# Feature products of one sample each on 32-column quarters, and one table gathered instead of three

## The chip, the cores and the metric

The kernel runs on one core of a Trainium2 chip. The metric is the device time of one execution in microseconds; the median of three runs of the kernel before is 417.11 us (416.43 to 417.47). The engines in the profile are PE (TensorE's matmuls), PEld (its weight loads, which can overlap the matmuls), DVE (VectorE), ACT (ScalarE), POOL (GpSimd) and SP (SyncE).

## The reference

For each of 2048 samples, 26 embedding rows of 128 numbers are looked up and set beside one dense row; all 351 pairwise dot products of these 27 vectors go, with the dense row, through a three-layer network.

```python
e = jnp.stack([tbl_0[ids[:, 0]], ..., tbl_25[ids[:, 25]]], axis=1)      # 2048 x 26 x 128
combined = jnp.concatenate([e, dense_x[:, None, :]], axis=1)            # 2048 x 27 x 128
interact = jnp.einsum('bfd,bgd->bfg', combined, combined)
z = interact[:, _TRIU_I, _TRIU_J]                                       # 351 pairs
h = jnp.concatenate([z, r_dense_x], axis=1)                             # 479
h = jnp.maximum(h @ W_top1 + b_top1, 0.0)                               # 512
h = jnp.maximum(h @ W_top2 + b_top2, 0.0)                               # 256
y = h @ W_top3
```

All inputs are float32. Seven tables have 1000 rows, ten 1250, eight 12500 and one 125000.

## The kernel before

The batch is worked on in 8 blocks of 256 samples, each of two tiles of 128. All features of a sample end up in `xt` (partitions: the 128 numbers of a row; free: sample, then feature slot, 32 slots for a sample). There are two ways into it.

**Gathered features.** POOL issues one indirect DMA for each (tile, table) (L577), which puts 128 table rows into `raw`. PE turns them with a transpose against `ident` (L594, `turn` steps, up to four tables in one PSUM bank), and ACT copies the bank into `xt` (L821). `SHARES` says how many of the ten small ("hot") tables are gathered in each block beside the 16 large ones: none in block 0, three in blocks 1 to 7. That makes 298 gathers.

**One-hot features.** The other hot tables lie in SBUF, cut into chunks of 128 rows (8 chunks for a table of 1000 rows, 10 for 1250), as a rounded part `hot_hi` and a residue `hot_lo`. DVE compares the block's ids with row numbers (L874, `onehot`, up to four chunks of 256 samples in one instruction, a ring of `RING = 3` such pieces), and PE multiplies each chunk by its one-hot columns (L613, one product with `hot_hi`, one with `hot_lo`; the first use of some tables takes `hot_in` as float32, `direct`). ACT copies the sum into `xt` (L387). Each table of a block is an "item", each item is two or three "pieces".

**Feature products.** For four samples at once PE takes the 128 columns of `xt` (four samples times 32 slots) as weights and the 4 x 27 columns as the moving side (L629). The result has 128 x 108 numbers, of which only the four diagonal blocks are wanted. Four such products fill a bank of `gram_ps` (two banks). `gram_copy` (L402 to L412) takes the four diagonal blocks out with four copies of 32 partitions, one for each sample of a group, on ACT; for the last tile two of the four are DVE's. A tile has 8 fills (`n_gram`), so 128 in all. A float32 matmul shows as two records and two weight loads in the trace, so 512 products are 1024 records.

**Tail.** For each block the pairs are turned and packed (L653, L424, L428), turned again (L661), and multiplied by the weights (L684, L690). In blocks 0 to 6 these steps are spread among the next block's steps; for the last block they come at the end (L712 to L775).

**What sets the order.** `order` is one list of steps (`hot`, `turn`, `gram`, `held`, `tail`), made from slots (L181 to L230). Every engine walks this same list and does its part of each step, waiting on semaphores for the others. `gram_slots` (L173) puts one fill of products and two slots of hot pieces in turn. `pieces_made` (L241) says after which step DVE makes which one-hot piece: at most `RING` ahead of use, one at a `gram` step. `copied_no` and `x_free` hold PE back until ACT has emptied one of three banks `x_ps`. POOL walks its own list of gathers: it waits for the landing of all but the last two gathers of the burst of eight before (`burst_landed`), and for the turn that frees its part of `raw`. The weights' rounding on ACT (`round_at`), their residue on DVE (`split_at`), and the residues of the direct tables (`split_late`) are hung on steps of the list.

## Time and profile before

| | |
|---|---|
| median of three runs | 417.11 us |
| the profiled execution | 417.3 us |
| its span, first to last instruction | 415.5 us |
| granted TensorE clock | 1.00 throughout |
| busy: PE / PEld | 393.7 us (95%) / 367.4 us (88%) |
| busy: POOL / ACT / DVE | 288.6 us (69%) / 264.6 us (64%) / 185.9 us (45%) |

Busy time is the union of an engine's records. A matmul's record reaches from its start to its modelled end, and the next one starts long before that, so the busy share says little about how fast PE goes; the distance between two starts does. It is worked out here from a timeline row of n records: (length of the row minus the length of one record) / (n - 1). POOL's busy time leaves out about 0.3 us between two gathers, in which it waits for nothing that the profile shows.

### The profile page before, as it was taken

How to read it: one execution, taken by the hardware profiler on the slowest of the kernel's cores; microseconds unless marked ns; L12 is line 12 of the kernel's file. 1: busy time of each engine (PE TensorE's matmuls, PEld its weight loads, DVE VectorE, ACT ScalarE, POOL GpSimd, SP SyncE). 2: the span in 40 equal slices, each digit the busy share in tenths (PEclk: the TensorE clock that was granted, in tenths of full speed). 3: DMA queues.
4: the chain of work that ended last, by engine and by line, in shares of the span. 5: the costliest groups of instructions: out<-in, count | busy, mean ns of one | idle time of the engine just before them, and what ended most of it. 6: DMA issues, size and time to landing. Idle time of an engine off the chain costs nothing.

```text
span 415.5 us, 8094 instructions
## 1 busy us (share of the span) xinstructions
PE 393.7 (95%) x3094; PEld 367.4 (88%) x3094; DVE 185.9 (45%) x216; ACT 264.6 (64%) x915; POOL 288.6 (69%) x306
## 2 busy tenths in 40 slices
PE   3899999999999999999999999999999999989997
PEld 2678899899899989998999989998999989889886
DVE  5796868441546224541447134451447124401142
ACT  2351377868586766767585766757485766866532
POOL 6776787777777777777777777777777777777000
PEclk9999999999999999999999999999999999999999
DMA  6788333212313222122222232312212222122000
GB/s 179 228 239 245 111 102 98 58 44 66 84 51 77 56 65 78 52 83 64 53 81 54 52 90 59 77 52 69 77 52 56 79 64 54 52 53 56 6 2 2
DMA packets 18231, 32.43 MB, mean 78 GB/s; under 512 B 6120, under 2 KB 9072, under 8 KB 18192
## 3 DMA queue, kind: packets, MB, share of 16 engines
q0 software_dynamic: 9536, 19.55, 18.3%
q1 hardware_dynamic: 7776, 11.57, 9.0%
q10 hardware_dynamic: 880, 0.80, 0.7%
q8 instruction: 25, 0.41, 0.4%
q14 instruction: 14, 0.11, 0.1%
HBM read 31.88 MB, written 0.01 MB: 77 GB/s over the span
## 4 chain that ended last, share of the span: by engine, by line
POOL 54%; issue 24%; PE 11%; DMA 9%; ACT 1%; POOLq 0%; ACTq 0%
POOL raw L577 54%; DMA raw<-in_tbl,ids_sb 9%; PE gram_ps L629 4%; PE tail_ps L684 2%; PE tail_ps L661 1%; PE tail_ps L653 1%; PE x_ps L721 1%; DMA ids_sb<-in_ids 1%; PE x_ps L594 1%; PE x_ps L613 0%; PE tail_ps L732 0%; PE x_ps L715 0%; PE x_ps L716 0%; PE x_ps L725 0%; PE gram_ps L774 0%
## 5 line engine op out<-in xcount | busy, mean ns | idle before, releaser
L577 POOL DMA_INDIRECT raw<-in_tbl,ids_sb x298 | 287.7, 966 | 95.3 <-issue 88.0
L874 DVE TENSOR_TENSOR onehot<-ids_wide,row_ps 128x1024 fp32r<-128x1024 int16 (+1 forms) x121 | 143.9, 1206 | 108.6 <-PE x_ps L613 107.7
L411 ACT COPY gram<-gram_ps 32x104 f32<-32x104 f32 x496 | 117.8, 237 | 46.0 <-PE gram_ps L629 38.3
L629 PE MATMUL gram_ps<-xt 128*128 128x108 f32 x1024 | 129.2, 276 | 2.2 <-ACT xt L821 1.0
L629 PEld LDWEIGHTS gram_ps<-xt 128*128 128x128 f32 x1024 | 121.9, 191 | 5.3 <-ACT gram L411 1.3
L613 PE MATMUL x_ps<-onehot,hot_hi 128*128 128x256 f32 x416 | 110.5, 299 | 7.4 <-ACT xt L387 6.4
L613 PE MATMUL x_ps<-onehot,hot_lo 128*128 128x256 f32 x416 | 103.2, 281 | 0.0
L613 PEld LDWEIGHTS x_ps<-onehot,hot_hi 128*128 128x128 f32 x416 | 78.4, 189 | 14.5 <-ACT xt L387 10.8
L613 PEld LDWEIGHTS x_ps<-onehot,hot_lo 128*128 128x128 f32 x416 | 78.6, 189 | 0.0
L387 ACT COPY xt<-x_ps 128x128 f32<-128x128 f32 (+1 forms) x80 | 36.0, 504 | 34.6 <-PE x_ps L613 34.1
L821 ACT COPY xt<-x_ps 128x512 f32<-128x512 f32 (+1 forms) x78 | 48.1, 679 | 1.3 <-PE x_ps L594 1.3
L594 PE MATMUL x_ps<-ident,raw 128*128 128x128 f32 x298 | 39.6, 275 | 1.1 <-DMA raw<-in_tbl,ids_sb 0.8
L613 PE MATMUL x_ps<-onehot,hot_in 128*128 128x256 f32 x124 | 30.1, 400 | 6.8 <-DMA hot_in<-in_tbl 6.8
L594 PEld LDWEIGHTS x_ps<-ident,raw 128*128 128x128 f32 x298 | 33.3, 141 | 3.1 <-ACT xt L821 1.5
L473 DVE TENSOR_TENSOR h_lo<-h,h_hi 128x256 fp32r<-128x256 f32 x28 | 12.0, 429 | 51.9 <-ACT h L445 51.8
L613 PEld LDWEIGHTS x_ps<-onehot,hot_in 128*128 128x128 f32 x124 | 24.4, 201 | 10.7 <-issue 7.3
L468 DVE TENSOR_TENSOR zt_lo<-tail_ps,zt_hi 118x256 fp32r<-118x256 f32 (+2 forms) x24 | 10.2, 424 | 40.3 <-ACT zt_hi L440 40.2
L684 PE MATMUL tail_ps<-zt_hi,weights_hi 118*128 118x256 f32 (+2 forms) x84 | 26.0, 336 | 0.0
L684 PE MATMUL tail_ps<-zt_hi,weights_lo 118*128 118x256 f32 (+2 forms) x84 | 21.7, 284 | 0.0
L424 ACT COPY z<-tail_ps 128x100 f32<-128x100 f32 (+12 forms) x99 | 13.5, 230 | 10.7 <-PE tail_ps L653 10.6
L444 ACT ACTIVATE h_hi<-tail_ps,b_sb 128x256 fp32r<-128x256 f32 x28 | 13.3, 475 | 9.8 <-PE tail_ps L684 9.0
L785 ACT CAST hot_hi<-hot_in 128x1024 fp32r<-128x1024 f32 x7 | 7.3, 1047 | 16.9 <-DMA hot_in<-in_tbl 16.9
(76 smaller groups left out, 317.6 us busy)
## 6 DMA issues: line engine op xcount, KB each, us to landing
raw<-in_tbl,ids_sb POOLq DMA_INDIRECT x298, 2.6
hot_in<-in_tbl SPq DMA_DIRECT2D x14, 256.0 KB, 3.3
ids_wide<-in_hot_ids SPq DMA_DIRECT2D x14, 256.0 KB, 3.4
hot_in<-in_tbl SPq DMA_DIRECT2D x6, 320.0 KB, 4.0
weights_in_place<-in_w SPq DMA_DIRECT2D x10, 128.0 KB, 2.7
dense_sb<-in_dense_t ACTq DMA_DIRECT2D x6, 128.0 KB, 2.5
dense_sb<-in_dense_t SPq DMA_DIRECT2D x2, 128.0 KB, 3.5
w1d_sb<-in_w SPq DMA_DIRECT2D x2, 128.0 KB
```

The source lines that it names most:

```text
L387: last = copy(xt[:, place:place + (b - a) * P, feature], src[:, a * P:b * P])
L411: last = copy(gram[rows, :, per_fill * i:per_fill * (i + 1)], src)
L424: copy(z[:, :, pair_start[q // 2]:pair_start[q // 2 + 1]], src)
L444: nc.scalar.activation(h1_hi[:, j, :], ps[:, 0:BLOCK], ACT.Relu, bias=bias).then_inc(h1_rounded, 1)
L473: nc.vector.tensor_tensor(h1_lo[:, j, :], h1[:, j, :], h1_hi[:, j, :].bitcast(F32), ALU.subtract).then_inc(h1_split, 1)
L577: nc.gpsimd.indirect_dma_start(out=raw[k][:, f, :], out_offset=None, in_=sources[f], in_offset=bass.IndirectOffsetOnAxis(ap=ids_sb[:, t, f ...
L594: last = nc.tensor.transpose(ps[:, c * P:(c + 1) * P], raw[k][:, f, :], ident[:, :])
L613: last = nc.tensor.matmul(ps, table[:, chunk_at[j] + c, :], moving[:, c - a, :], start=(c == 0 and table is tables_of[0]), stop=(c == chun ...
L629: last = nc.tensor.matmul(gram_ps[m % 2][:, col:col + QUAD * feats], xt[:, b:b + QUAD, :].rearrange("p b f -> p (b f)"), xt[:, b:b + QUAD, ...
L684: last = nc.tensor.matmul(ps[:, 0:BLOCK], weights, moving, start=(n == 0), stop=(n == len(products_of) - 1))
L821: copy(xt[:, b:b + P, fs[0]:fs[-1] + 1], src).then_inc(x_copied, 1)
L874: nc.vector.tensor_tensor(columns(p), ids_wide[:, it // IDS % IDS_RING, it % IDS, 0:width].unsqueeze(1).to_broadcast([P, n, width]), row_n ...
```

## The change

A product now takes one sample: 27 columns of `xt` as weights, 26 as the moving side, and its result goes to partitions 32s to 32s+26 of the bank for the sample s of its group of four, so that it uses one 32-column quarter of the array. There are 2048 such products, 4096 records. A bank now holds 16 groups (16 x 26 = 416 columns), a tile has 2 fills, and one copy of 128 partitions takes a whole fill (for the last tile one of 64 partitions on ACT and one on DVE). The rows that no product writes are set to 0 once by DVE, in the two PSUM banks, where before unused slots of `xt` were. The hot pieces among the products stand in two stretches for a tile.

`SHARES` goes from 3 to 1 for blocks 1 to 7: 270 gathers instead of 298, and two more hot tables of 1250 rows (20 chunks) by one-hot products in each of these seven blocks. `pieces_made` may make three pieces at a `gram` step. The residues of the direct tables and the splits of the weights hang on other `gram` steps.

```diff
--- before.py
+++ after.py
@@ -14,10 +14,11 @@
 BLOCK = 256
 SLOTS = 32
 QUAD = 4
+FILLS = 2
 BANK = 512
 HOT = 10
 DIRECT = 5
-SHARES = (0, 3, 3, 3, 3, 3, 3, 3)
+SHARES = (0, 1, 1, 1, 1, 1, 1, 1)
 MOST = max(SHARES)
 RAW = 2
 DENSE = 2
@@ -83,9 +84,9 @@
         count = -(-n // 4)
         turn_groups.append([list(range(g * n // count, (g + 1) * n // count)) for g in range(count)])
     most_turns = max(len(gs) for gs in turn_groups)
-    per_fill = BANK // (QUAD * feats)
-    n_gram = groups // per_fill
-    assert n_gram * per_fill == groups
+    per_fill = groups // FILLS
+    n_gram = FILLS
+    assert per_fill * (feats - 1) <= BANK
     gram_block = tiles_block * n_gram
 
 
@@ -172,8 +173,8 @@
 
     def gram_slots(t, hot=()):
 
-        return [[("gram", t * n_gram + i)] + [step for slot in hot[(i - 1) * len(hot) // n_gram:(i + 1) * len(hot) // n_gram]
-                                              for step in slot if i % 2] for i in range(n_gram)]
+        cut = [i * len(hot) // n_gram for i in range(n_gram + 1)]
+        return [[("gram", t * n_gram + i)] + [step for slot in hot[cut[i]:cut[i + 1]] for step in slot] for i in range(n_gram)]
 
 
 
@@ -247,7 +248,7 @@
             end = min(used + RING + 1, len(pieces))
             coming = [s[0] for s in order[n + 1:] if s[0] in ("gram", "hot")][:1]
             if step[0] == "gram":
-                end = min(end, nxt + 1)
+                end = min(end, nxt + 3)
             elif coming == ["gram"]:
                 end = nxt
             made.append(list(range(nxt, max(nxt, end))))
@@ -319,7 +320,7 @@
 
         second = [("gram", gram_block + n) for n in range(len(weight_parts) - n_kz)]
         round_at = [("hot", item_start[nh + 2 + n]) for n in range(n_kz)] + second
-        split_at = [("gram", n_gram + 1 + 2 * n) for n in range(n_kz)] + second
+        split_at = [("gram", n_gram + n // 2) for n in range(n_kz)] + second
 
         x_ps = [psum(f"x_ps{b}", [P, BANK]) for b in range(3)]
         row_ps = psum("row_ps", [P, BANK])
@@ -346,13 +347,13 @@
         consts_ready = sem("consts_ready")
         hot_rounded = sem("hot_rounded")
         hot_split = sem("hot_split")
-        xt_cleared = sem("xt_cleared")
         row_no_ready = sem("row_no_ready")
         piece_ready = sem("piece_ready")
         piece_used = sem("piece_used")
         turn_full = [sem(f"turn_full{k}") for k in range(RAW)]
         x_copied = sem("x_copied")
         dense_copied = sem("dense_copied")
+        gram_cleared = sem("gram_cleared")
         gram_full = sem("gram_full")
         gram_copied = sem("gram_copied")
         gram_shared = sem("gram_shared")
@@ -404,12 +405,9 @@
             h, i = divmod(m, gram_block)
             if i == 0:
                 reach(eng, tail_full["cols"], h * n_cols)
-            for s in quads:
-                rows = slice(32 * s, 32 * s + 32)
-                src = gram_ps[m % 2][rows, 0:per_fill * QUAD * feats].rearrange(
-                    "p (g c) -> p c g", g=per_fill)[:, s * feats:(s + 1) * feats - 1, :]
-                last = copy(gram[rows, :, per_fill * i:per_fill * (i + 1)], src)
-            last.then_inc(done, 1)
+            rows = slice(SLOTS * quads[0], SLOTS * (quads[-1] + 1))
+            src = gram_ps[m % 2][rows, 0:per_fill * (feats - 1)].rearrange("p (g c) -> p c g", g=per_fill)
+            copy(gram[rows, :, per_fill * i:per_fill * (i + 1)], src).then_inc(done, 1)
 
         def product_copied(eng, m):
 
@@ -623,12 +621,14 @@
                     pe.wait_ge(x_copied, max(copied_no[step] for step in of_tile))
                     pe.wait_ge(dense_copied, t // tiles_block + 1)
                 product_copied(pe, m - 2)
+                if m == 0:
+                    pe.wait_ge(gram_cleared, len(gram_ps))
                 for g in range(per_fill):
-                    b = t % XT * P + (i * per_fill + g) * QUAD
-                    col = g * QUAD * feats
-                    last = nc.tensor.matmul(gram_ps[m % 2][:, col:col + QUAD * feats],
-                                            xt[:, b:b + QUAD, :].rearrange("p b f -> p (b f)"),
-                                            xt[:, b:b + QUAD, 0:feats], start=True, stop=True)
+                    cols = slice(g * (feats - 1), (g + 1) * (feats - 1))
+                    for s in range(QUAD):
+                        b = t % XT * P + (i * per_fill + g) * QUAD + s
+                        last = nc.tensor.matmul(gram_ps[m % 2][SLOTS * s:SLOTS * s + feats, cols],
+                                                xt[:, b, 0:feats], xt[:, b, 0:feats - 1], start=True, stop=True)
                 last.then_inc(gram_full, 1)
 
             def tail_has(kind, h):
@@ -787,8 +787,6 @@
             def hot_copy(it):
                 j, first, n = items[it]
                 act.wait_ge(piece_used, item_end[it])
-                if it == 0:
-                    act.wait_ge(xt_cleared, 1)
 
                 to_xt(copy, first, n, nf + j, x_ps[fill_no["hot", it] % len(x_ps)]).then_inc(x_copied, 1)
                 if it == (it - j_th[it] + last_item[first] + 1) // 2:
@@ -881,19 +879,20 @@
             for n in row_kinds:
                 copy(row_no[n], row_sb[n][:, :]).then_inc(row_no_ready, 1)
             dve.wait_ge(row_no_ready, len(row_kinds))
-            nc.vector.memset(xt[:, :, feats:], 0.0).then_inc(xt_cleared, 1)
+            for ps in gram_ps:
+                nc.vector.memset(ps[:, :], 0.0).then_inc(gram_cleared, 1)
             for (kind, *what), made in zip(order, pieces_made()):
                 if kind == "tail":
                     h, key, part = what
                     if part == parts[key] - 1:
                         tail_split(dve, h, key)
                 elif kind == "gram":
-                    if what[0] < len(split_late):
-                        hot_residue(split_late[what[0]])
+                    if what[0] < n_gram:
+                        for j in split_late[what[0] * len(split_late) // n_gram:(what[0] + 1) * len(split_late) // n_gram]:
+                            hot_residue(j)
                     if what[0] >= shared_from:
                         gram_copy(dve, copy, gram_shared, (2, 3), *what)
-                    if (kind, *what) in split_at:
-                        n = split_at.index((kind, *what))
+                    for n in [n for n, at in enumerate(split_at) if at == (kind, *what)]:
                         hi, lo, src = weight_parts[n]
                         dve.wait_ge(weights_rounded, n + 1)
                         nc.vector.tensor_tensor(lo, src, hi.bitcast(F32), ALU.subtract).then_inc(weights_split, 1)
```

**PE, one-hot products and feature products in block 0's second tile.** L613 are one-hot products, L629 feature products of four samples. Before:

```order
L613 MATMUL x_ps<-onehot,hot_lo 128x256
L629 MATMUL gram_ps<-xt 128x108 x8
L613 MATMUL x_ps<-onehot,hot_hi 128x256
L613 MATMUL x_ps<-onehot,hot_lo 128x256
L613 MATMUL x_ps<-onehot,hot_hi 128x256
L613 MATMUL x_ps<-onehot,hot_lo 128x256
L613 MATMUL x_ps<-onehot,hot_hi 128x256
L613 MATMUL x_ps<-onehot,hot_lo 128x256
L613 MATMUL x_ps<-onehot,hot_hi 128x256
L613 MATMUL x_ps<-onehot,hot_lo 128x256
L629 MATMUL gram_ps<-xt 128x108 x8
L613 MATMUL x_ps<-onehot,hot_hi 128x256
```

After, from the middle of the same place (L611 are one-hot products, L630 feature products of one sample):

```order
L611 MATMUL x_ps<-onehot,hot_lo 128x256
L611 MATMUL x_ps<-onehot,hot_hi 128x256
L611 MATMUL x_ps<-onehot,hot_lo 128x256
L630 MATMUL gram_ps<-xt 27x26 x64
L611 MATMUL x_ps<-onehot,hot_hi 128x256
L611 MATMUL x_ps<-onehot,hot_lo 128x256
L611 MATMUL x_ps<-onehot,hot_hi 128x256
L611 MATMUL x_ps<-onehot,hot_lo 128x256
L611 MATMUL x_ps<-onehot,hot_hi 128x256
L611 MATMUL x_ps<-onehot,hot_lo 128x256
L611 MATMUL x_ps<-onehot,hot_hi 128x256
```

Eight products of four samples stood between eight one-hot products; now 64 products of one sample stand in one run, with 24 one-hot products between two runs.

**PE, second tile of a later block, at the end of the z transposes (L661).** Before:

```order
L629 MATMUL gram_ps<-xt 128x108 x4
L661 MATMUL tail_ps<-ident,z 118x64 x4
L629 MATMUL gram_ps<-xt 128x108 x4
L661 MATMUL tail_ps<-ident,z 128x64 x4
L661 MATMUL tail_ps<-ident,z 105x64 x4
L629 MATMUL gram_ps<-xt 128x108 x4
L661 MATMUL tail_ps<-ident,z 64x64 x4
L629 MATMUL gram_ps<-xt 128x108 x8
```

After:

```order
L661 MATMUL tail_ps<-ident,z 128x64 x4
L661 MATMUL tail_ps<-ident,z 105x64 x4
L630 MATMUL gram_ps<-xt 27x26 x64
L661 MATMUL tail_ps<-ident,z 64x64 x4
L630 MATMUL gram_ps<-xt 27x26 x64
L592 MATMUL x_ps<-ident,raw 128x128 x3
```

The tile's two runs of 64 products have four transposes between them, and no one-hot products.

**ACT, copies out of PSUM in a first tile (L411 and L410: feature products; L387 and L388: one-hot sums).** Before:

```order
L387 COPY xt<-x_ps 128x256
L411 COPY gram<-gram_ps 32x26x4 x16
L387 COPY xt<-x_ps 128x256
L387 COPY xt<-dense_sb 128x256
L411 COPY gram<-gram_ps 32x26x4 x16
```

After:

```order
L388 COPY xt<-x_ps 128x256
L410 COPY gram<-gram_ps 128x26x16
L388 COPY xt<-x_ps 128x256
L388 COPY xt<-dense_sb 128x256
L410 COPY gram<-gram_ps 128x26x16
```

Sixteen copies of 32 partitions between two other copies became one of 128 partitions.

## Rows read from the trace of the kernel before

**Rows 1.** The page: granted clock in tenths by slice, and the chain by engine.

```profile
PEclk9999999999999999999999999999999999999999
...
POOL 54%; issue 24%; PE 11%; DMA 9%; ACT 1%; POOLq 0%; ACTq 0%
```

**Rows 2.** Windows: stretch, length, busy us of PE, PEld, DVE, ACT, POOL, clock, DMA, GB/s.

```profile
152.00:204.00 52.00, 50.85 (x418) 47.67 (x416) 21.92 (x23) 35.05 (x120) 39.19 (x43) 1.00 0.24 66
204.00:256.00 52.00, 50.85 (x422) 48.46 (x421) 22.43 (x24) 35.26 (x129) 39.50 (x42) 1.00 0.25 68
```

**Rows 3.** Timeline of PE: start, length, form, count [idle before]; one place, two blocks.

```profile
195.94 0.39 PE L613 MATMUL x_ps<-onehot,hot_hi 128*128 128x256 f32 x1 [0.92 <-ACT xt L387]
...
243.09 0.39 PE L613 MATMUL x_ps<-onehot,hot_hi 128*128 128x256 f32 x1 [0.92 <-ACT xt L387]
```

**Rows 4.** Timeline of POOL, near the end; the third is the last gather.

```profile
377.20 0.94 POOL L577 DMA_INDIRECT raw<-in_tbl,ids_sb  x1 [0.30 <-issue]
378.45 0.95 POOL L577 DMA_INDIRECT raw<-in_tbl,ids_sb  x1 [0.30 <-issue]
...
383.62 1.11 POOL L577 DMA_INDIRECT raw<-in_tbl,ids_sb  x1 [0.30 <-issue]
```

**Rows 5.** Timeline of PE, the last tile's products and what follows.

```profile
390.76 7.57 PE L629 MATMUL gram_ps<-xt 128*128 128x108 f32 x64 [0.96 <-ACT xt L821]
398.17 0.62 PE L715 MATMUL x_ps<-b_sb,ident 128*128 128x256 f32 x2
```

**Rows 6.** Timeline of PE, two fills among one-hot products.

```profile
157.83 0.28 PE L613 MATMUL x_ps<-onehot,hot_lo 128*128 128x256 f32 x1
157.95 1.93 PE L629 MATMUL gram_ps<-xt 128*128 128x108 f32 x16
159.65 0.37 PE L613 MATMUL x_ps<-onehot,hot_hi 128*128 128x256 f32 x1
159.85 0.28 PE L613 MATMUL x_ps<-onehot,hot_lo 128*128 128x256 f32 x1
```

**Rows 7.** Lines by form, whole span: form, count | busy us, mean ns | idle before.

```profile
L874 DVE TENSOR_TENSOR onehot<-ids_wide,row_ps 128x1024 fp32r<-128x1024 int16 x115 | 138.3, 1220 | 106.8 <-PE x_ps L613 105.8 <-DMA ids_wide<-in_hot_ids 0.6 <-issue 0.2
L629 PE MATMUL gram_ps<-xt 128*128 128x108 f32 x1024 | 129.2, 276 | 2.2 <-ACT xt L821 1.0 <-ACT xt L387 0.7 <-ACT gram L411 0.5
L629 PEld LDWEIGHTS gram_ps<-xt 128*128 128x128 f32 x1024 | 121.9, 191 | 5.3 <-ACT gram L411 1.3 <-ACT xt L821 1.2 <-ACT xt L387 0.9
L411 ACT COPY gram<-gram_ps 32x104 f32<-32x104 f32 x496 | 117.8, 237 | 46.0 <-PE gram_ps L629 38.3 <-PE tail_ps L653 1.4
...
L821 ACT COPY xt<-x_ps 128x512 f32<-128x512 f32 x64 | 42.3, 715 | 1.3 <-PE x_ps L594 1.3
L594 PE MATMUL x_ps<-ident,raw 128*128 128x128 f32 x298 | 39.6, 275 | 1.1 <-DMA raw<-in_tbl,ids_sb 0.8 <-issue 0.3
...
L613 PE MATMUL x_ps<-onehot,hot_in 128*128 128x256 f32 x124 | 30.1, 400 | 6.8 <-DMA hot_in<-in_tbl 6.8
...
L387 ACT COPY xt<-x_ps 128x256 f32<-128x256 f32 x38 | 23.2, 611 | 26.2 <-PE x_ps L613 25.9
...
L821 ACT COPY xt<-x_ps 128x384 f32<-128x384 f32 x14 | 7.2, 517 | 0.0
...
L874 DVE TENSOR_TENSOR onehot<-ids_wide,row_ps 128x768 fp32r<-128x768 int16 x6 | 5.7, 953 | 1.9 <-PE x_ps L613 1.9
...
L661 PE MATMUL tail_ps<-ident,z 64*64 64x64 f32 x32 | 3.3, 223 | 0.0
...
L661 PEld LDWEIGHTS tail_ps<-ident,z 64*64 64x64 f32 x32 | 2.0, 108 | 0.9
...
L690 PEld LDWEIGHTS tail_ps<-h,w_sb 128*1 128x1 f32 x28 | 1.8, 82 | 2.9 <-issue 0.2
```

**Rows 8.** Timeline of PE, three other forms.

```profile
85.64 0.41 PE L661 MATMUL tail_ps<-ident,z 64*64 64x64 f32 x4
...
152.83 1.51 PE L594 MATMUL x_ps<-ident,raw 128*128 128x128 f32 x12
```

## The prediction

> **What bounds the kernel now.** I read the page first: the granted clock is full in all slices, and the chain that ended last is 54% POOL and 24% "issue", which is the pause between gathers [rows 1]. That reads as a kernel bound by POOL. The windows say that PE is as full: 50.85 of 52 us in two stretches of the steady part, while ACT has 35 and DVE 22 [rows 2]. The timeline settles how the two stand. The same place of two consecutive blocks is at 195.94 and 243.09 us, so a block takes 47.15 us, and the largest wait of PE in it is 0.92 us, for a copy of ACT [rows 3]. POOL issues a gather every 1.25 us (377.20 to 378.45) [rows 4]; a block's 2 x 19 gathers take 47.5 us. So both bound: PE without room, POOL without room. After the last gather (383.62 us) PE still has the last tile: its products begin at 390.76 and end at 398.17, and the final tail follows [rows 4, 5].
>
> A change gains only if it takes time from both. This one takes gathers from POOL, gives PE the one-hot products in their stead, and pays PE with the feature products. The price of a small feature product is the whole question.
>
> **Part by part.** The sum is made against the profiled execution, 417.3 us (span 415.5 and 1.8 around it), 0.2 above the median of 417.11.
>
> *Removed: 1024 product records.* Sixteen take 1.93 us with a record's length of 0.276 [rows 6, 7]: (1.93 - 0.276) / 15 = 0.110 us from start to start. 1024 x 0.110 = 113 us of PE.
>
> *Added: one-hot products.* Two tables of 10 chunks in 7 blocks are 140 chunks, each two products, 0.12 us apart (157.83 to 157.95) [rows 6]: 140 x 2 x 0.12 = 33.6 us on PE. DVE makes 140 x 0.305 = 43 us more of one-hot columns (1.220 us for four chunks) [rows 7], ACT 14 more copies of 0.611 [rows 7], 8.6 us.
>
> *Removed: 28 gathers and transposes.* POOL: 28 x 1.25 = 35.0 us [rows 4]. PE: twelve transposes take 1.51 us, one record 0.275 [rows 7, 8], so 0.112 each, 28 x 0.112 = 3.1 us.
>
> *Added: 4096 small records.* The trace shows no product on a quarter of the array, so I bound it. Streaming: eleven records of 256 float32 columns take 2.54 us with 0.400 each [rows 7, 8], (2.54 - 0.400) / 10 = 0.214 apart or 0.84 ns for a column; 26 columns are 22 ns. Weights: a load of 128 columns lasts 191 ns, of one column 82 [rows 7]: 0.86 ns for a column, 27 columns are 23 ns beyond what any load has. Loads run beside matmuls now (PEld busy 121.9 of PE's 129.2 us in these products [rows 7]), and each record is set by the longer of the two: 128 x 0.86 = 110 ns, the measured distance, against 91 ns for 108 columns of streaming.
> - Upper end of this sort: everything in one line at the nearest distance in the trace. Four z transposes of 64 columns take 0.41 us, one 0.223 [rows 7, 8]: 0.062. 4096 x 0.062 = 254 us.
> - In one line, loads hidden: 23 ns and some 2 ns between records, 0.025: 102 us.
> - Lower end: four quarters fully beside each other, 25 / 4 = 6 ns: 26 us.
> - What I take: the two records of one product go to the same quarter and must follow each other (25 ns), the next product goes to another quarter and starts beside the second of them, 3 ns later. A product then costs 28 ns, a record 14. 4096 x 0.014 = 57.3 us. I choose it because the instructions come in that order and nothing in the rows says that one quarter has to wait for another's stream, but no row shows the overlap either.
>
> The Trainium skill has figures for this. Its page "TensorE: Matmul & The Clock Gate", section "Part 3: Packing small matmuls — row/col tiling", says that matmuls at different tile positions start about 4 ns apart, by which a product would be 25 + 4 = 29 ns; as an estimate 59 us instead of 57.3. The same section says a weight load overlaps a running matmul only if its row group differs, and here all products use all four row groups. No run here shows that for quarters. For the full array the trace disagrees: load and matmul of the same rows do overlap, 121.9 beside 129.2 us busy [rows 7].
>
> *Switching.* After a fill pair the first one-hot product stands 0.20 before the next (159.65, 159.85) where 0.12 is usual [rows 6]: 0.08 lost at each of over 100 stretches of products, which become 30. That returns some 7 us. Entering and leaving a mode with quarters is not in the trace; at 0.1 to 0.2 us each way it takes 6 to 12. I put both together at 0, with -5 to +6.
>
> *ACT and the copies.* 496 copies of 0.237 (117.8 us [rows 7]) become 30 of 128 x 416. Copies of 384 and 512 columns take 0.517 and 0.715 [rows 7], so about 0.56 each, 17 us. That is 100 us off ACT, but ACT waits for PE in this kernel (38.3 of its 46.0 us idle at these copies [rows 7]); what PE waits for ACT is at most 0.92 us at a time, once a block [rows 3], so some 7 us. Worth 0 to -8 us, as much as is not given back to DVE, next.
>
> *DVE.* A steady block needs 16 pieces of 1.220 and 4 of 0.953 [rows 7], 23.3 us, where it needed 14 (17.1). Of these, 16 lie between two tails, some 19 us of DVE in about 22 us of PE. A piece (1.22) takes longer than its eight products (0.94), so in a run of 24 products PE eats the ring of three ahead of DVE, and the products' run lets DVE catch up. Cover is thin: a stall of 0.5 to 1 us a block where it fails, 4 to 7 in all. With ACT's gain I put the pair at 0, with -6 to +7.
>
> *At nothing:* two PSUM clears for one of `xt`, before the first table has come (6.8 us of waiting for it [rows 7]); residues and splits on other steps, DVE work beside products, at most 3 us once if one-hot pieces of block 1 come late; two more roundings on ACT, 2 us in a freed engine.
>
> Sum: 417.3 - 113.0 + 33.6 - 3.1 + 57.3 + 0 = 392.1. POOL alone would allow 417.3 - 35.0 - 3.8 (the last tile's products 3.6 instead of 7.4 us after the last gather [rows 5]) = 378.5. PE's sum is later, so PE bounds. Forecast: **392**.
>
> **Rivals.**
> 1. *Quarters truly beside each other.* Records 6 to 9 ns. PE's sum is 334.8 + 26 to 37 = 361 to 372, below POOL's 378.5, and DVE gets no time to catch up: **378**, gathers every 1.25 us to the end. For it: weights and streams of different quarters touch different columns and banks' partitions. Against: the two records of a product share a quarter.
> 2. *One line (slower).* At each product of L630 the next record starts only when the stream before it is through; place: all 30 product runs on PE, price 4096 x 0.025 = 102 us: 334.8 + 102.4 = **437**. It decides from 20 ns a record: 334.8 + 82 = 417. For it: every distance in the trace is that of one line, and records run in order. By the skill's same page, section "Wait — 56ns, not 53.3ns?", starts never come closer than about 25 ns however few the columns. The shortest distance in this trace is 62 ns with 64 columns [rows 8], so it neither agrees nor disagrees.
> 3. *Loads not hidden.* If a quarter's load waits for the stream, a record costs 23 + 22 = 45 ns or, by the z transposes, up to 62: 184 to 254 us, total **519 to 589**. Against: loads are hidden in every row of the same kind now [rows 7].
> 4. *The clock.* Runs of 64 to 128 products keep few columns at work. If the granted clock left 1.00 [rows 1] for 1.2 GHz in them, their 57 us would double: **449**. Every row has it at full rate, also where short transposes stand, and one-hot products surround most runs.
> 5. *Near no change.* Stalls on DVE, instruction supply in the runs, or switches that cost 20 us more than I have: **412 to 420**.
>
> **How the numbers follow.** Forecast (record 12 to 17 ns, 383 to 404): 0.40. Rival 1: 0.21. Rival 2: 0.23. Rival 3: 0.07. Rival 4: 0.03. Rival 5: 0.06, a third of it within 0.3%, which is about what a measurement of this kernel can tell from no change. Faster: 0.40 + 0.21 + 0.03 = 0.64; same 0.02; slower 0.34. The range goes from 375 (rival 1 with 3 us to spare) to 441 (rival 2 with 4), leaving out rivals 3 and 4 and the edges, some 0.17. The forecast's own range is 383 to 404.
>
> **What would show it.** In the profile after: the products' line with 4096 records, 64 of a fill's product pairs (128 records) in about 1.8 us plus one record's length; 3.2 us is rival 2, 0.9 rival 1, 6 and more rival 3. 266 to 272 gathers at 1.25 us, the last at about 350 us if POOL never waits, with new waits of POOL for turns if PE bounds. A block at 44 us for the forecast (47.15 - 14.1 + 4.8 - 0.4 + 7.2 = 44.6, less a wait), 42.5 if POOL bounds (34 x 1.25), 50 for rival 2. ACT's gram copies near 0.56 us. The clock row full. DVE busy near 230 us; waits of PE for DVE on `onehot` would mean that the cover was too thin. The prediction is wrong first of all if the distance of two small records isn't near 14 ns.

## The result: 404 us, and the profile after

The changed kernel takes 404.47 us (median; before in the same runs 417.29). The ratio to the kernel before is 0.969, 95% interval 0.965 to 0.973: 3% faster. One of its four executions (411.54 us) spent longer at the lower clock and is left out of the ratio. The forecast was 392, the range 375 to 441; 404.47 lies just above the forecast's own narrower range (383 to 404) and below that of rival 5 (412 to 420).

The page of the changed kernel (span 401.4 us, the execution itself 403.16): busy time with count, granted clock in tenths by slice, the queue that brings PE's instructions (requests, MB, share), the chain by engine.

```profile
span 401.4 us, 14335 instructions
...
PE 360.7 (90%) x6418; PEld 330.1 (82%) x6418; DVE 223.7 (56%) x247; ACT 169.4 (42%) x473; POOL 259.0 (65%) x278
...
PEclk9998999999999969999999999997899999999999
...
q8 instruction: 51, 0.84, 0.8%
...
PE 75%; DVE 8%; DMA 8%; issue 7%; ACT 1%; SPq 0%; DVEq 0%; ACTq 0%
```

POOL has left the chain ([rows 1] had it at 54%) and PE has taken it, as forecast. Two things are new: the clock row has gaps (mean clock 0.979, so about 17 us at half rate), and the instruction queue has 51 parts instead of the 25 of before:

```profile
q8 instruction: 25, 0.41, 0.4%
```

Lines by form of the changed kernel; [rows 7] has those of before.

```profile
L872 DVE TENSOR_TENSOR onehot<-ids_wide,row_ps 128x1024 fp32r<-128x1024 int16 x129 | 152.8, 1217 | 74.2 <-PE x_ps L611 71.3 <-DMA ids_wide<-in_hot_ids 1.4 <-DVE zt_lo L466 1.1
L611 PE MATMUL x_ps<-onehot,hot_hi 128*128 128x256 f32 x566 | 148.3, 297 | 7.1 <-issue 4.0 <-ACT xt L388 2.4 <-DVE hot_lo L858 0.4
...
L630 PE MATMUL gram_ps<-xt 128*27 128x26 f32 x4096 | 53.0, 193 | 21.5 <-issue 18.2 <-ACT xt L819 1.0
L630 PEld LDWEIGHTS gram_ps<-xt 128*27 128x27 f32 x4096 | 44.1, 105 | 30.5 <-issue 24.5 <-ACT xt L819 1.2
...
L410 ACT COPY gram<-gram_ps 128x416 f32<-128x416 f32 x30 | 15.2, 507 | 64.2 <-PE gram_ps L630 64.2
```

The small products are cheap: PE is busy with them for 53.0 us where it was for 129.2. But 21.5 us of idle time stand before them, 18.2 of it "issue", time in which PE waits for nothing that the profile shows. In [rows 7] the products had 2.2.

Timeline of PE, product runs of two tiles (start, length, form, count, [idle before]):

```profile
112.68 1.83 PE L630 MATMUL gram_ps<-xt 128*27 128x26 f32 x128
...
117.50 1.51 PE L630 MATMUL gram_ps<-xt 128*27 128x26 f32 x124
120.26 0.24 PE L630 MATMUL gram_ps<-xt 128*27 128x26 f32 x4 [1.26 <-issue]
...
134.76 1.76 PE L630 MATMUL gram_ps<-xt 128*27 128x26 f32 x128
138.46 0.38 PE L661 MATMUL tail_ps<-ident,z 64*64 64x64 f32 x4 [1.93 <-issue]
138.77 1.87 PE L630 MATMUL gram_ps<-xt 128*27 128x26 f32 x124
142.18 0.30 PE L630 MATMUL gram_ps<-xt 128*27 128x26 f32 x4 [1.54 <-issue]
```

128 records last 1.83 us, one of them 0.187: (1.83 - 0.187) / 127 = 12.9 ns from start to start. The run at 117.50 stops after 124 records and goes on 1.26 us later; the transposes at 138.46 wait 1.93 us, the rest of the run at 142.18 waits 1.54. None of these waits has an engine as its releaser.

The block's time, from the start of the first product run of four blocks in a row (the rows are cut off by their windows; only the start is read):

```profile
162.54 0.64 PE L630 MATMUL gram_ps<-xt 128*27 128x26 f32 x54
...
207.55 1.12 PE L630 MATMUL gram_ps<-xt 128*27 128x26 f32 x106
...
251.86 0.42 PE L630 MATMUL gram_ps<-xt 128*27 128x26 f32 x32
...
299.92 0.48 PE L630 MATMUL gram_ps<-xt 128*27 128x26 f32 x35
```

(299.92 - 162.54) / 3 = 45.8 us a block, against 47.15 before [rows 3] and 44.6 in the forecast.

Where PE's time went, as the sum of the distances from each record's start to the next. A distance between two records of one kind stands in that kind's row, one into or out of a product run in the second row, and every other change of kind in the fifth; a distance over 0.9 us counts as 0.2, and the rest as gap. Worked out from the start times of all PE records, us:

| | before | after | four fills | eight fills | one quarter | pairs on halves |
|---|---|---|---|---|---|---|
| within product runs | 108.4 | 49.9 | 46.2 | 40.8 | 112.4 | 61.5 |
| into and out of product runs | 19.4 | 9.4 | 16.6 | 31.3 | 8.8 | 18.2 |
| one-hot products | 123.6 | 156.9 | 156.0 | 157.4 | 154.8 | 156.3 |
| transposes of gathers | 29.7 | 26.7 | 26.1 | 26.2 | 26.0 | 26.0 |
| tail, other changes of kind | 114.9 | 121.2 | 120.0 | 115.6 | 119.0 | 117.1 |
| gaps | 10.4 | 28.0 | 17.6 | 9.8 | 5.6 | 5.8 |

Before to after: -58.5 - 10.0 + 33.3 - 3.0 + 6.3 + 17.6 = -14.3, the 14.1 us between the spans.

### The profile page after: what moved, and what is told of

It reads as the page before. It is cut to its first block, busy times and chain, and to the rows that moved or that the text cites. A ratio compares the mean times of both kernels' runs of the same rounds, so it can differ in the third digit from the quotient of the medians.

```text
span 401.4 us, 14335 instructions
## 1 busy us (share of the span) xinstructions
PE 360.7 (90%) x6418; PEld 330.1 (82%) x6418; DVE 223.7 (56%) x247; ACT 169.4 (42%) x473; POOL 259.0 (65%) x278
## 4 chain that ended last, share of the span: by engine, by line
PE 75%; DVE 8%; DMA 8%; issue 7%; ACT 1%; SPq 0%; DVEq 0%; ACTq 0%
PE x_ps L611 31%; PE tail_ps L684 16%; PE gram_ps L630 12%; PE x_ps L592 8%; DMA hot_in<-in_tbl 8%; DVE onehot L872 7%; PE tail_ps L661 2%; PE tail_ps L653 2%; PE tail_ps L690 2%; DVE hot_lo L858 1%; PE x_ps L721 1%; PE tail_ps L732 0%; DVE zt_lo L466 0%; PE x_ps L715 0%; PE x_ps L716 0%
## 5 line engine op out<-in xcount | busy, mean ns | idle before, releaser
L575 POOL DMA_INDIRECT raw<-in_tbl,ids_sb x270 | 258.1, 956 | 92.7 <-issue 78.9
L872 DVE TENSOR_TENSOR onehot<-ids_wide,row_ps 128x1024 fp32r<-128x1024 int16 (+1 forms) x163 | 183.9, 1161 | 88.3 <-PE x_ps L611 85.4
L611 PE MATMUL x_ps<-onehot,hot_hi 128*128 128x256 f32 x566 | 148.3, 297 | 7.1 <-issue 4.0
L611 PE MATMUL x_ps<-onehot,hot_lo 128*128 128x256 f32 x566 | 141.6, 284 | 0.0
L611 PEld LDWEIGHTS x_ps<-onehot,hot_hi 128*128 128x128 f32 x566 | 108.2, 191 | 11.9 <-issue 5.6
L611 PEld LDWEIGHTS x_ps<-onehot,hot_lo 128*128 128x128 f32 x566 | 108.5, 192 | 1.6 <-issue 1.6
L630 PE MATMUL gram_ps<-xt 128*27 128x26 f32 x4096 | 53.0, 193 | 21.5 <-issue 18.2
L388 ACT COPY xt<-x_ps 128x128 f32<-128x128 f32 (+1 forms) x100 | 45.6, 514 | 61.8 <-PE x_ps L611 61.0
L630 PEld LDWEIGHTS gram_ps<-xt 128*27 128x27 f32 x4096 | 44.1, 105 | 30.5 <-issue 24.5
L410 ACT COPY gram<-gram_ps 128x416 f32<-128x416 f32 (+1 forms) x32 | 16.2, 506 | 68.3 <-PE gram_ps L630 68.3
L819 ACT COPY xt<-x_ps 128x384 f32<-128x384 f32 (+1 forms) x78 | 44.5, 631 | 1.3 <-PE x_ps L592 1.3
L592 PE MATMUL x_ps<-ident,raw 128*128 128x128 f32 x270 | 39.1, 280 | 0.0
L592 PEld LDWEIGHTS x_ps<-ident,raw 128*128 128x128 f32 x270 | 31.1, 143 | 2.2 <-ACT xt L388 1.1
L611 PE MATMUL x_ps<-onehot,hot_in 128*128 128x256 f32 x104 | 25.4, 401 | 7.0 <-DVE onehot L872 7.0
L611 PEld LDWEIGHTS x_ps<-onehot,hot_in 128*128 128x128 f32 x104 | 20.6, 204 | 10.3 <-issue 7.5
L684 PE MATMUL tail_ps<-zt_hi,weights_hi 118*128 118x256 f32 (+2 forms) x84 | 26.9, 348 | 0.0
L684 PE MATMUL tail_ps<-zt_hi,weights_lo 118*128 118x256 f32 (+2 forms) x84 | 21.7, 284 | 0.0
L684 PE MATMUL tail_ps<-dense_sb,w1d_sb 128*128 128x256 f32 x56 | 17.4, 393 | 0.0
```

The lines of the kernel that those rows point to most:

```text
L388: last = copy(xt[:, place:place + (b - a) * P, feature], src[:, a * P:b * P])
L410: copy(gram[rows, :, per_fill * i:per_fill * (i + 1)], src).then_inc(done, 1)
L575: nc.gpsimd.indirect_dma_start(out=raw[k][:, f, :], out_offset=None, in_=sources[f], in_offset=bass.IndirectOffsetOnAxis(ap=ids_sb[:, t, f ...
L592: last = nc.tensor.transpose(ps[:, c * P:(c + 1) * P], raw[k][:, f, :], ident[:, :])
L611: last = nc.tensor.matmul(ps, table[:, chunk_at[j] + c, :], moving[:, c - a, :], start=(c == 0 and table is tables_of[0]), stop=(c == chun ...
L630: last = nc.tensor.matmul(gram_ps[m % 2][SLOTS * s:SLOTS * s + feats, cols], xt[:, b, 0:feats], xt[:, b, 0:feats - 1], start=True, stop=True)
```

## Experiments

Two theories stood after the result. **Supply:** PE's instructions come in parts of 16 KB (0.84 MB in 51). The page has 2 x 6418 matmuls and loads for these 0.84 MB, and the page before 2 x 3094 for 0.41 MB, some 65 bytes each, so about 250 in a part; a run of 64 products is 256 of them and lasts about 1.7 us, so PE runs dry. **Its rivals:** the gaps come with the quarters or the banks, once for so many products; and the small products by themselves lower the clock.

In the trace of the changed kernel PE has 14 distances over 0.9 us in or shortly behind product runs, 24.4 us together. A request of that queue starts 2.3 to 2.6 us before the end of each of the 14, and none in the 4 us before the end of any of PE's four other distances of that size. Examples are the requests at 117.64 for the one that ends at 120.26, 136.03 for 138.46, 139.60 for 142.18 and 230.26 for 232.80. For the first the window from 117.6 to 117.7 shows it:

```profile
q8 instruction: 1, 0.02, 75.1%
```

### The products alone

```diff
-SHARES = (0, 1, 1, 1, 1, 1, 1, 1)
+SHARES = (0, 3, 3, 3, 3, 3, 3, 3)
```

> The changed kernel with three tables gathered again in blocks 1 to 7 (298 gathers); the small products stay. Theory: both old limits were at 47 us a block, so relieving PE alone gives little. POOL's 298 gathers at 1.25 us end at 384 us as before, and only the last tile's products (7.4 us before, about 3.5 and one stall of 2 now) get shorter: 411 to 415 us. PE's stalls in the product runs should cost nothing here, since PE has some 9 us of room in each block: POOL's gaps stay 0.30 us. Rival: PE's stalls reach POOL through the freeing of raw; then POOL shows waits for PE and the time is 417 us or more.

413.51 us, ratio 0.991 (0.988 to 0.995). In the range; the changed products alone bring 1%, because POOL's 298 gathers take as long as they did: the last starts at 386.4 us (383.6 before). PE now waits for gathers at their transposes (L592) in each block:

```profile
ACT xt L819 <- PE x_ps L592: 41.0, 17, 4.8
PEld x_ps L592 <- issue: 35.7, 11, 4.6
PE x_ps L592 <- DMA raw<-in_tbl,ids_sb: 25.9, 9, 4.4
```

POOL waits for PE for only 0.6 us in all, so these waits don't hold up the gathers, but the clock falls behind them: its mean is 0.942.

```profile
core 0: 412.4 us, clock 0.942
```

This run also bears on the gaps. It has the same 4096 product records on four quarters, in runs of the same size, and of the 14 gaps over 0.9 us in or behind product runs two are left, of 0.95 and 1.68 us. Idle time before the products with "issue" as releaser is 2.9 us, where it was 18.2:

```profile
PE gram_ps L630 <- issue: 2.9, 4, 1.5
```

A gap that came once for so many products would be there all the same. One of supply needn't be, since instructions can come while PE waits for gathers.

### The shares alone

```diff
-SHARES = (0, 3, 3, 3, 3, 3, 3, 3)
+SHARES = (0, 1, 1, 1, 1, 1, 1, 1)
```

(in the kernel before)

> The kernel before with one table gathered instead of three from block 1 on; the products of four samples stay. Theory: PE is full, so 140 chunks x 2 x 0.12 us = 33.6 us less 3.1 us of transposes come on top: 447 us. Rival: before was bound by POOL and PE had hidden room; then 417 us less up to 35, about 385 to 400.

441.75 us, ratio 1.060 (1.058 to 1.062). PE was full before; two tables more by one-hot products cost 25 us, 5 less than 33.6 - 3.1. Counted as in the table above, PE's gaps went from 10.4 to 4.9 us, which makes up those 5. POOL now waits for PE:

```profile
POOL raw L577 <- PE x_ps L594: 36.2, 17, 5.6
```

Neither half is worth much without the other: 0.991 and 1.060 give 0.969 together, because each takes time from one of two bounds.

### Half of the products

```diff
-                    for s in range(QUAD):
+                    for s in range(0, QUAD, 2):
```

This leaves out every second sample's products, so the result is incomplete.

> The changed kernel with the products of every second sample left out (1024 instead of 2048), runs of 32 with 128 instructions. Theory (instruction supply): hardly any idle gap over 1 us in product runs, PE is relieved of 26 us of records and some 20 us of gaps, POOL bounds: 377 to 382 us, clock 1.00. Rival (gaps come once per run, whatever it holds): as many gaps as in the full one, 14 or so, and 390 us or more. Distance of two records: if records of one product wait for each other and different quarters overlap, the two quarters left give the same 6 to 8 ns at a run's start.

373.66 us (one execution), under the range. In place of 14 gaps of over 0.9 us in or behind product runs there is one, of 1.0 us, with a request 2.7 us before its end; the instruction queue brings 35 parts. Another wait of 3.5 us, behind block 0's first tile, is for DVE, which makes three residues in a row (3.75 us) before the next `onehot`; that one is my "at most 3 us once". The clock wasn't full (0.986), since PE stood still there and, further on, for gathers. The distance came out as a surprise:

```profile
126.74 1.07 PE L630 MATMUL gram_ps<-xt 128*27 128x26 f32 x64
```

(1.07 - 0.187) / 63 = 14.0 ns between records of two quarters, where four quarters start 7 ns apart (the median distance in the changed kernel). So 14 ns isn't a fixed step between records.

### All products on one quarter

```diff
-                        last = nc.tensor.matmul(gram_ps[m % 2][SLOTS * s:SLOTS * s + feats, cols],
+                        last = nc.tensor.matmul(gram_ps[m % 2][0:feats, cols],
```

The four samples of a group overwrite each other here; number and size of the instructions stay.

> The changed kernel with every product written to the first quarter's partitions (0 to 26), so that the four samples of a group overwrite each other; number and size of all instructions unchanged, three quarters of the feature products are lost. Theory from the runs so far (7 ns between records on four quarters and 14 on two at the start of a run, so a quarter takes a record every 28 ns and the quarters fully overlap): 28 ns from record to record throughout, 4096 x (28 - 12.7) = 63 us more, less the gaps of supply (256 instructions then last 3.6 us, longer than a part of 16 KB takes to come), 20 to 25 us, and what the clock took, up to 8: 430 to 447 us. Rival (7 ns is only how the start of queued records shows, and the pace is one of the instruction supply, 12 ns): as the changed kernel, 400 to 408 us.

437.88 us (one execution), in the theory's range and far above the rival's 400 to 408. Timeline of PE, one fill:

```profile
116.29 3.70 PE L630 MATMUL gram_ps<-xt 128*27 128x26 f32 x128
```

(3.70 - 0.187) / 127 = 27.7 ns. A quarter takes a record every 28 ns; two make it 14, four 7. Quarters overlap fully, both records of a product included. The same number of instructions, in the same 51 parts, now runs without one gap in the products, and at full clock:

```profile
PEclk9999999999999999999999999999999999999999
...
q8 instruction: 51, 0.84, 0.8%
```

```profile
L630 PE MATMUL gram_ps<-xt x4096: 187/187/208, 50.2 to 418.6; 128*27 128x26 f32 x196
...
its engine sat idle before it (us, times) until:
  ACT xt L819: 1.0, 1
  ACT h L842: 0.4, 1
```

This decides against rivals that tie the gaps or the clock to small products as such, since these are equally many in the same runs. What changed is that a run's 256 instructions last 3.6 us instead of 1.7. By itself it leaves open that using four quarters at once brings the gaps; the run with the products alone, above, and the one with eight fills, below, have all four quarters and hardly any.

The Trainium skill, page "TensorE: Matmul & The Clock Gate", section "Part 3: Packing small matmuls — row/col tiling", says that a weight load overlaps a running matmul only if its row group differs. All products here use the same rows, and 28, 14 and 7 ns on one, two and four quarters disagree with that.

### Four fills, eight fills

```diff
-FILLS = 2
+FILLS = 4
```

> The changed kernel with FILLS = 4: four runs of 32 products a tile instead of two of 64, with one-hot products or tail steps between most of them; twice as many copies on ACT, each half as long. Theory (instructions arrive in parts of 16 KB, 256 of them, each some 2.3 us after it is asked for; a run of 64 products uses 256 in 1.8 us and runs dry): runs of 128 instructions with others between them run dry less often. The 14 idle gaps of 1 to 2 us in or after product runs fall to 6 or fewer, the granted clock stays above 0.99, time 383 to 392 us. Rival (a gap belongs to the quarters or to the banks, once per so many products): as many gaps of the same length, 400 to 406 us. Rival (small products by themselves lower the clock): gaps fall but the clock stays near 0.98, 392 to 398 us.

393.17 us, ratio 0.942 (0.939 to 0.944), one us outside the range, and faster than the changed kernel by 3%. The gaps over 0.9 us in or behind product runs go from 14 (24.4 us together) to 10 (14.2 us), not to 6: in each block one tile's four runs still stand almost together, 64 products in one. Idle time before product records by releaser "issue" (us, times), changed kernel and four fills:

```profile
  issue: 18.2, 12
```

```profile
  issue: 11.8, 11
```

The mean clock:

```profile
core 0: 392.0 us, clock 0.991
```

A run of 64 records is also quicker in itself:

```profile
110.40 0.74 PE L630 MATMUL gram_ps<-xt 128*27 128x26 f32 x64
```

(0.74 - 0.187) / 63 = 8.8 ns, against 12.9 in a run of 128. In the changed kernel the first 32 records of a run follow each other at 7 to 8 ns, the next 96 at 11 to 17 (distances over 0.9 us left out). Why a longer run slows down before it is dry isn't settled.

> The changed kernel with FILLS = 8: runs of 16 products. Theory (instruction supply, and about 0.2 us for going into and out of the quarters at each run): fewer gaps than with four fills (14, of which 9 in or right behind runs after the first block's start), but some 60 more changes of mode, 0.1 to 0.2 us each: 388 to 396 us, within 1% of four fills. Rival (changes of mode drain the array and are dear): over 400 us.

With `FILLS = 8`: 394.85 us, ratio 0.950 (0.948 to 0.952), within 1% of four fills. "Issue" before product records:

```profile
  issue: 3.3, 6
```

Two gaps are left of 14, 3.2 us together, but 91 runs instead of 52 have 31.3 us of going in and out instead of 16.6, with 5.4 us less inside the runs. That is 0.34 us for each run, in and out together. It is a gross price: all rows of the table but the gaps grew by 6.4 us for these 39 runs, 0.16 us for each, because shorter runs go faster inside and the other rows give up the distances at the new borders.

### Two samples a product, on halves

```diff
-FILLS = 2
+FILLS = 4
+PAIR = 2
...
-                    for s in range(QUAD):
+                    for s in range(0, QUAD, PAIR):
...
-                        last = nc.tensor.matmul(gram_ps[m % 2][SLOTS * s:SLOTS * s + feats, cols],
-                                                xt[:, b, 0:feats], xt[:, b, 0:feats - 1], start=True, stop=True)
+                        last = nc.tensor.matmul(gram_ps[m % 2][SLOTS * s:SLOTS * (s + PAIR), cols],
+                                                xt[:, b:b + PAIR, :].rearrange("p b f -> p (b f)"),
+                                                xt[:, b:b + PAIR, 0:feats - 1], start=True, stop=True)
```

(with four copies of 32 partitions for a fill and the unused slots of `xt` set to 0, as before the change)

> Two samples a product on 64-column halves of the array: 1024 products, 2048 records of 64 columns of weights and 52 moving, four fills a tile, four copies of 32 partitions for a fill (256 in all). All pairs are computed. Half the instructions in the product runs. Theory (supply is what leaves the gaps; a half takes a record every 55 to 60 ns, the two halves overlap, so 28 to 30 ns between records, 57 to 61 us in all against 52): the gaps of over 1 us in product runs go, the clock stays full, 379 to 388 us, near the 378 that POOL allows. Rival (gaps come with quarters or halves, not with the supply): 398 us or more. Rival (halves don't overlap as quarters do): 55 ns between records, 115 us: 425 us or more.

396.33 us, ratio 0.953 (0.951 to 0.955). The supply behaved as expected and the time was missed. Half the product instructions, 35 parts:

```profile
q8 instruction: 35, 0.57, 0.6%
```

One fill:

```profile
113.25 1.14 PE L633 MATMUL gram_ps<-xt 128*64 128x52 f32 x32
```

(1.14 - 0.221) / 31 = 29.6 ns for two halves, as expected. No gap of supply is left, the clock is full, and PE has no room at all (window: length, busy PE, PEld, DVE, ACT, POOL, clock):

```profile
145.00:190.00 45.00, 44.95 (x548) 42.05 (x547) 25.80 (x28) 28.41 (x87) 33.99 (x37) 1.00 0.28 73
190.00:235.00 45.00, 44.95 (x548) 42.03 (x546) 25.79 (x28) 28.39 (x92) 33.04 (x35) 1.00 0.27 69
```

My 379 to 388 subtracted all gaps and the clock's loss from the changed kernel's time, and left out most of what the products cost more: 11.6 us inside the runs and 8.8 for going in and out, of which the other rows give back 5.4. So 15.0 us more stand against 22.2 us less of gaps. PE's own sum bounds, not POOL.

### Two tables gathered in some blocks

```diff
-FILLS = 2
+FILLS = 4
...
-SHARES = (0, 1, 1, 1, 1, 1, 1, 1)
+SHARES = (0, 2, 1, 2, 1, 2, 1, 1)
```

> Four fills a tile, and two tables gathered in blocks 1, 3 and 5 instead of one (SHARES 0, 2, 1, 2, 1, 2, 1, 1). With four fills the last gather starts at 348 us of a span of 392 and PE is full, so PE bounds. Theory: 30 chunks less on PE, 60 x 0.12 = 7.2 us, six transposes more, 0.7; six gathers more for POOL, 7.5 us, which has them free: 385 to 389 us. Rival (the gaps of supply and the clock move with every shift of the order, and outweigh 7 us): 390 us or more.

390.84 us, ratio 0.938 (0.935 to 0.941).

> Four fills a tile, and two tables gathered in blocks 1 to 4, one in blocks 5 to 7. Theory: 40 chunks less on PE, 9.6 us, less 0.9 of transposes: 382 to 387 us, POOL's last gather near 358 us and not yet the bound. Rival: gathers of the early blocks now hold PE up (two tables in a row of blocks, 36 gathers x 1.25 = 45 us a block against PE's 44), and the sum is no better than with three blocks: 387 to 391 us.

With `(0, 2, 2, 2, 2, 1, 1, 1)`: 392.37 us, ratio 0.942 (0.940 to 0.945). Both miss their ranges: against four fills alone (0.939 to 0.944) neither is told apart. The one-hot products got 7.5 us shorter, as reckoned (148.5 instead of 156.0), but the gaps grew from 17.6 to 19.6 and 22.7 us, and the mean clock fell from 0.991 to 0.983 and 0.974. In the second, four of the gaps, 1.4 to 3.5 us, stand at transposes of gathers between 143 and 212 us, as its rival had it, though its time lies above that rival's 387 to 391 us too. The best version is four fills, with or without this.

## Why the prediction was right, and where its steps were not

- **What bounds.** Right. PE and POOL were both full: the shares alone made it 25 us slower, the products alone 3 us faster. After the change PE bounds; the last gather starts at 351.6 us, 350 forecast.
- **Removed products, added one-hot products, transposes.** The table has 108.4 us inside the runs against 113, +33.3 against +33.6 and -3.0 against -3.1. These rows leave out every distance at which the kind changes. With each distance counted to the earlier record's kind, the removed products were 117.0 us, the one-hot products went from 137.4 to 173.9 (+36.5), the transposes from 35.4 to 30.8 (-4.6), and the rest from 106.2 to 105.5.
- **The small record.** The size was right and its reason wrong, so that part was luck. 14 ns were forecast, 12.9 measured in a whole run; 49.9 us inside the runs, 53.8 with the distances behind them, against 57.3. I had the two records of a product in one line, and the next product beside the second only. In fact the four quarters run fully beside each other at 28 ns a quarter, as in rival 1, which gives 7 ns; runs of 128 records don't hold that pace, and that brought the average near my 14. The 0.84 ns for a streamed column came from a row of eleven records that [rows 8] doesn't show; sixteen such records at 14.68 us in the trace of before last 3.69 us, 0.219 apart, which gives the same 22 ns for 26 columns. Rival 2 (one line) is what the one-quarter kernel did, at 27.7 ns and 438 us; it was forecast at 25 ns and 437.
- **Switching.** Put at 0, -5 to +6, and near that. The row of going in and out fell by 10.0 us, but mostly because 29 runs have fewer borders than 78, and a border's distance holds what the earlier record takes anywhere (0.12 us for a one-hot record). What lies above the median distance of the earlier record's kind there, the first distance behind a run included, was 6.1 us before and is 7.9 after: +1.8.
- **The step that failed: the instruction supply.** It was named in rival 5 and stood in the sum at nothing. It costs 21.6 us in 14 gaps (24.4 from start to start); the other waits over 0.9 us went from 10.4 to 6.4 us, so net +17.6. What the clock lost behind these gaps comes on top. The view for it was on the page: 25 parts of the instruction queue in 415 us, 2 x 4096 small instructions to come where 2 x 1024 were, and a run of 256 in my own 1.8 us. I didn't divide.
- **The clock.** Rival 4 had it fall in the product runs. It fell at 37.5, 139.9 and 276.5 us, each time behind waits of PE of about 2 to 2.7 us (a wait for a copy of ACT at 33.3, then gaps of supply), but not behind every such wait: not behind the one of 2.17 us at 186.7. Windows of 2 us of the changed kernel (length, PE busy and records, clock):

```profile
134.00:136.00 2.00, 1.92 (x113) 1.00 0.22 47
136.00:138.00 2.00, 0.45 (x27) 1.00 0.28 74
138.00:140.00 2.00, 1.50 (x114) 0.98 0.18 41
140.00:142.00 2.00, 0.64 (x34) 0.50 0.27 61
142.00:144.00 2.00, 1.82 (x12) 0.50 0.19 45
144.00:146.00 2.00, 2.00 (x9) 0.50 0.25 66
146.00:148.00 2.00, 2.00 (x14) 0.81 0.13 33
148.00:150.00 2.00, 2.00 (x19) 1.00 0.26 66
```

PE is idle for most of 136 to 138 and of 140 to 142; the clock goes to half (1.2 GHz) at 140 and stays there until after 146, in tail and one-hot products without a gap. With one quarter the same number of records ran at 1.00 to the end. Some 17 us at half rate cost up to 8.5 us (an estimate: at full clock the same work would take half of that time), spread over the table's rows.
- **DVE, ACT.** The thin cover held: DVE busy 223.7 us (230 forecast), and the only wait of PE for `onehot` is the first. ACT's copies take 0.507 us (0.56 forecast).
- **The sum.** Forecast 392.1. Counted by the earlier record's kind, the products took 63.2 us less (117.0 to 53.8) where 55.7 were forecast: -7.5. The one-hot products cost +2.9 over their 33.6, the transposes gave 1.5 more than their 3.1, the rest gave 0.7, and the gaps cost 17.6. That gives 402.9 of the 403.2 measured. How much of it is the clock isn't separated. The distance from forecast to result is the gaps' term, and what hid a part of it is that the products gained more than forecast.

## What to carry to other kernels

Small products on quarters of the array cost as little as a quarter of their time each (28 ns a record on one, 7 ns on four at a run's start, 12.9 over a run of 128 records), but then PE uses up 256 instructions in less than two microseconds, and a part of its instructions takes 2.3 to 2.6 to come: divide the instructions of a run by the part, and break up runs that hold one. Don't break them finer than needed: a run costs some 0.3 us to enter and leave, and still 0.16 when the faster pace inside shorter runs is set against it. When two engines are both full, a change has to take from both, and each half of it looks useless alone.

## What was not expected of the hardware

- The time that the supply costs has no engine's name: the profile calls it "issue". It can also come after the small products that used the instructions up: with two tables gathered in blocks 1, 3 and 5 the trace has such a gap at the tail's products (L684), 1.05 us idle before 313.10, with a request 2.7 us before its end. The kernel before has no wait that needs it: at 361.01 a part was asked for and PE went on at 363.26, but the gather that it waited for had landed 0.14 us before that.
- The Trainium skill, page "Runtime: NRT & Kernel Launch", section "Instruction fetch mechanics", says that instructions come in blocks of 16 KB, 256 of them, which agrees with 0.84 MB in 51 parts, and that their fetch is hidden, because a sequencer dispatches slower than its memory is filled. It isn't hidden where PE starts a load and a matmul every 7 to 13 ns: 14 gaps, 24.4 us.
- The clock fell to half behind some waits of PE of about 2 us, and stayed there longer than PE had been idle, with PE full (136 to 148 us above). Where PE waits for gathers in each block, as with the products alone, that happens in each block (mean clock 0.942).
